# Moving one chunk's refinement, attention and third norm into the gate stage, with the gates' PSUM banks shared out anew

## The reference, cut to what matters

```python
x = x + tanh(g_xattn[0]) * attention16heads(layernorm(x), ctx)        # 1st norm
n = layernorm(x)                                                       # 2nd norm of the code: norm 1
integrated, v = n, 0
for _ in range(2):                                                     # it = 0, 1
    h = gelu([integrated, v] @ w1 + b1)        # 8 experts of 64, and a shared one
    a, b, g = split(h @ w2 + b2)               # for the shared and the two chosen experts
    v_next = sigmoid(a) * v - softplus(b) * (integrated - mu)
    x_next = integrated + 0.1 * sigmoid(g) * v_next
    (weighted over shared, first, second; then mixed in by halt)
refined = gelu(integrated @ refine_w1 + b) @ refine_w2 + b
x = x + tanh(g_ffn[0]) * (n + integration_weight * refined)
n = layernorm(x)                                                       # norm 2
x = x + tanh(g_xattn[1]) * softmax(n @ ctx.T) @ ctx                    # one head, per sequence
n = layernorm(x)                                                       # norm 3
top2 experts of 8 by n @ Wr + br; x = x + tanh(g_ffn[1]) * sum_k w_k * (silu(n@W1+b1) * (n@W2+b2)) @ W3 + b3
```

## Time and profile before

| | |
|---|---|
| median of 3 runs | 653.5 us (652.99 to 660.25) |
| the profiled execution's own time | 653.35 us |
| its span | 651.5 us |
| TensorE matmuls busy | 567.6 us, 87% |
| VectorE busy | 431.5 us, 66% |
| ScalarE busy | 307.7 us, 47% |
| GpSimd busy | 205.1 us, 31% |
| mean granted TensorE clock | 0.925 of full |

### The profile page before, as it was taken

One profiled execution on the slowest core, in us unless ns is written; L12 is line 12 of the kernel. 1 busy time (PEld: TensorE's weight loads), 2 busy tenths in 40 slices (PEclk: granted clock), 3 DMA queues, 4 the chain that ended last, 5 costly groups with the idle time before them and its releaser, 6 DMA issues.

```text
span 651.5 us, 9912 instructions
## 1 busy us (share of the span) xinstructions
PE 567.6 (87%) x3307; PEld 339.3 (52%) x3318; DVE 431.5 (66%) x1054; ACT 307.7 (47%) x630; POOL 205.1 (31%) x214
## 2 busy tenths in 40 slices
PE   3777799898898689899999999999767498999994
PEld 2433434444453234344444444445646498999993
DVE  3778858888438888877624567676767754454455
ACT  2544446565667653445445244362634244444431
POOL 3909500101012679100572000001046673333330
PEclk9795869999999989899999999999888599999996
DMA  8595880000019700000004000000202399999966
GB/s 252 149 186 104 150 183 14 2 4 3 2 63 309 248 0 1 2 0 0 0 1 129 0 1 1 0 2 0 16 12 83 116 304 305 323 328 321 345 210 202
DMA packets 53894, 71.14 MB, mean 109 GB/s; under 512 B 11484, under 2 KB 41508, under 8 KB 53556
## 3 DMA queue, kind: packets, MB, share of 16 engines
q1 hardware_dynamic: 50852, 65.55, 35.0%
q0 software_dynamic: 2272, 4.69, 1.9%
q10 hardware_dynamic: 720, 0.27, 0.2%
HBM read 59.12 MB, written 21.29 MB: 123 GB/s over the span
## 4 chain that ended last, share of the span: by engine, by line
PE 42%; DVE 9%; SPq 7%; issue 3%; DMA 3%; ACT 2%; POOL 0%; POOLq 0%; DVEq 0%; ACTq 0%
PE psum L1871 19%; PE psum L2099 5%; PE psum L1800 3%; PE psum L1802 3%; SPq L571 2%; PE psum L1868 2%; PE psum L2110 2%; DMA wb<-in_wall_dram 2%; DVE hidden L1238 1%; PE psum L1960 1%; SPq L587 1%; SPq L581 1%; PE psum L1924 1%; SPq L578 1%; PE psum L1869 1%
## 5 line engine op out<-in xcount | busy, mean ns | idle before, releaser
L1871 PE MATMUL psum<-hidden,ew 128*128 128x512 f32 x320 | 145.5, 598 | 0.5
L830 ACT ACTIVATE probs<-psum 128x512 f32<-128x512 f32 x128 | 72.7, 596 | 60.9 <-PE psum L1659 60.2
L1871 PEld LDWEIGHTS psum<-hidden,ew 128*128 128x128 f32 x320 | 61.4, 192 | 71.7 <-issue 70.5
L1097 DVE TENSOR_REDUCE negmax<-psum 128x4 f32<-128x1024 f32 x64 | 77.0, 1218 | 23.0 <-PE psum L1636 22.8
L1566 DVE SCALAR_TENSOR_TENSOR gated<-psum,wb,silu_g 128x128 f32<-128x128 f32 x156 | 43.9, 345 | 54.6 <-ACT silu_g L1017 53.0
L2099 PE MATMUL psum<-xbT,wb 128*128 128x128 f32 x624 | 78.2, 280 | 0.8 <-DMA wb<-in_wall_dram 0.5
L2099 PEld LDWEIGHTS psum<-xbT,wb 128*128 128x128 f32 x624 | 74.4, 195 | 1.9 <-DMA wb<-in_wall_dram 1.2
L1017 ACT ACTIVATE silu_g<-psum,wb 128x128 f32<-128x128 f32 x156 | 44.5, 368 | 58.4 <-PE psum L2099 58.4
L773 POOL DMA_INDIRECT sorted_y<-yb,xb x39 | 37.2, 953 | 65.1 <-DVE yb L1558 63.6
L1659 PE MATMUL psum<-stacks 50*128 50x256 bf16 x256 | 49.5, 295 | 9.2 <-ACT probs L830 3.9
L631 POOL TENSOR_SCALAR rstd<-meanvar 128x4 f32<-128x4 f32 x16 | 4.9, 306 | 166.7 <-DVE meanvar L1035 166.6
(11 more groups left out here) (253 smaller groups left out, 994.4 us busy)
## 6 DMA issues: line engine op xcount, KB each, us to landing
wb<-in_wall_dram SPq DMA_DIRECT2D x39, 516.0 KB, 4.7
wb<-in_wall_dram SPq DMA_DIRECT2D x39, 256.0 KB, 4.9
sorted_x<-in_slots_dram SPq DMA_DIRECT2D x1, 9815.0 KB, 32.2
stacks<-stacked SPq DMA_DIRECT2D x12, 384.0 KB, 8.3
xb<-sorted_x SPq DMA_DIRECT2D x39, 65.0 KB, 3.7
stacked<-parts SPq DMA_DIRECT2D x6, 384.0 KB, 3.4
back<-sorted_y SPq DMA_DIRECT2D x8, 256.0 KB, 4.4
stacked<-parts SPq DMA_DIRECT2D x6, 256.0 KB, 3.4
```

Source lines behind the costliest of these rows:

```text
L830: nc.scalar.activation(probs[:, g % 2, h % 4, :, :], s2[n % 2].rearrange("p (k q) -> p k q", k=2), ACT.Exp, scale=float(HD) ** -0.5).then_ ...
L1097: nc.vector.tensor_reduce(negmax[:, p].rearrange("p h q -> p (h q)"), psum[:, i:i + 2, :].rearrange("p h (q k) -> p (h q) k", q=2), AX.X, ...
L1871: last = nc.tensor.matmul(dst, ew2[:, j, cols], hidden[:, k - 1, j, c, :], start=False, stop=(j == 3))
```

## The change

Norm 3 of chunk 0 now comes ahead of norm 2 of chunk 1 (`TURNS`). In the second iteration:

- `refine_up(0)` goes behind part 5 of chunk 1's gates, its Gelus to the start of chunk 2 on ScalarE, `refine_down(0)` between the soft units 1 and 2 of chunk 2, the rest of norm 2, the transposes and both scores of chunk 0 among the gates of chunk 2, and its maxima just ahead of the last two passes of `second_step(2)`.
- The transposes of chunk 0's probabilities stand behind soft units 1 and 2 of chunk 3, `weigh_context(0)` and (1) behind gate part 1, `rows_to_columns(0)` behind part 4. `refine_up(1)` and `refine_down(1)` stay behind parts 0 and 2; `second_columns(1)` behind part 5.
- The soft units of the second iteration have two banks, 2 and 3, and unit `u` waits for `soft_done` of unit `u - 2`. Bank 4 takes chunk 0's transposed probabilities, its attention output and its rows.
- The list behind the loop is shorter and in another order; VectorE's `choose(1)` goes ahead of `layer_norm_apply(2)`.
- The hidden units lie by chunk, so that the later stages' memory can be loaded once chunks 0 and 1 are through their gates; `wo` moves behind `attnT`; SyncE waits for four more semaphores ahead of the first expert's weights.

```diff
-TURNS = ((2, 0), (2, 1), (3, 0), (3, 1), (2, 2), (2, 3), (3, 2), (3, 3))
+TURNS = ((2, 0), (3, 0), (2, 1), (3, 1), (2, 2), (2, 3), (3, 2), (3, 3))
...
-        hidden = sm("hidden", [P, 2, 4, NC, CH])
+        hidden = sm("hidden", [P, NC, 2, 4, CH])
...
             if part == "up":
-                return bank[(0 if c < 2 else 6) + m]
+                return bank[m if c < 2 else (6, 2)[m]]
...
+        def soft_bank(it, c, k):
+
+            return bank[2 + (3 * c + k) % (2 if it else 3)]
+
+        def fused_bank(b):
+
+            return bank[4][:, b * 2 * D:(b + 1) * 2 * D] if b < 2 else bank[4 + b % 2][:, 0:2 * D]
+
+        def rows_bank(c):
+
+            return bank[(4, 5, 6, 6)[c]]
...
@@ SyncE
-            sp.wait_ge(gate_psum, gate_use(1, NC))
+            sp.wait_ge(gate_psum, gate_use(1, 2))
...
+            sp.wait_ge(gate_psum, gate_use(1, NC))
+            sp.wait_ge(state_ready, 2 * NC)
+            sp.wait_ge(refine_h_ready, 2 * NC)
+            sp.wait_ge(refined_psum, NC)
             sp.wait_ge(early_ready, 1)
             load_weights(0)
...
@@ GpSimd
             rstd_of_chunk(2, 0)
+            rstd_of_chunk(3, 0)
             rstd_of_chunk(2, 1)
...
+            rstd_of_chunk(3, 1)
+            send_rows(0, range(0, 2))
             rstd_of_chunk(2, 2)
-            send_rows(0, range(0, 4))
+            send_rows(0, range(2, 5))
             rstd_of_chunk(2, 3)
-            send_rows(0, range(4, GR))
-            send_rows(1, range(0, 3))
+            send_rows(0, range(5, GR))
+            send_rows(1, range(0, 5))
             rstd_of_chunk(3, 2)
-            send_rows(1, range(3, 6))
+            send_rows(1, range(5, GR))
             rstd_of_chunk(3, 3)
-            send_rows(1, range(6, GR))
...
@@ ScalarE
+                    if it and c == L and k == 1:
+                        copy_probsT(0)
...
-                    if it and c == L and i in (3, 5):
-                        copy_xT2(i // 5)
+                    if it and c == 2 and i == 3:
+                        copy_xT2(0)
+                    if it and c == L and i == 4:
+                        copy_xT3(0)
+                        copy_rows(0)
+                    if it and c == L and i == 5:
+                        copy_xT2(1)
...
-                    if it and c == L:
+                    if it and c == 2:
                         refine_gelus(0)
                     nc.scalar.preload_act_table_set("natural_log_exp_and_others")
+                    if it and c == L:
+                        exps2(0)
+                        exps2(1)
                     softplus(it, c)
                     if it and c == L:
+                        copy_probsT(1)
                         refine_gelus(1)
                     sigmoids(it, c)
...
@@ VectorE, second_step
-                if c == L:
+                if c == 2:
                     layer_norm_apply(0, turn(2, 0))
-                    add_refined(1)
                 for k in range(3):
+                    if c == L and k == 1:
+                        sums_of(0)
+                        fuse(0)
+                        fuse(1)
+                        third_stats(0)
                     dve.wait_ge(sigmoid_done, gate_use(1, c) + 2 + k)
...
                 if c == L:
-                    layer_norm_apply(1, turn(2, 1))
+                    add_refined(1)
+                    layer_norm_rows(0)
                 for k in range(3):
-                    if c == L and k:
-                        maxima2(k - 1)
+                    if c == L and k == 1:
+                        layer_norm_apply(1, turn(2, 1))
+                    if c == L and k == 2:
+                        maxima2(2)
+                        maxima2(3)
                     dve.wait_ge(sigmoid_done, gate_use(1, c) + 5 + k)
...
-                if c == L:
-                    maxima2(2)
-                    sums_of(0)
-                    maxima2(3)
+                if c == 2:
+                    maxima2(0)
+                    maxima2(1)
...
@@ VectorE, behind the loop
-            fuse(0)
-            fuse(1)
-            third_stats(0)
+            choose(0)
             sums_of(1)
             fuse(2)
-            layer_norm_rows(0)
             fuse(3)
             third_stats(1)
-            add_refined(2)
-            choose(0)
-            layer_norm_rows(1)
             weights_of(0)
             slots_of(0)
+            layer_norm_rows(1)
+            add_refined(2)
             add_refined(3)
+            choose(1)
             layer_norm_apply(2, turn(2, 2))
-            choose(1)
             maxima2(4)
...
@@ TensorE, soft_parts
-                    if u >= 3:
+                    if it and 3 * c + k >= 2:
+                        pe.wait_ge(soft_done, u - 1)
+                    elif u >= 3:
                         pe.wait_ge(soft_done, u - 2)
-                    controller(bank[2 + u % 3][:], k, 1, c).then_inc(soft_psum, 1)
-                    if it and c == L and k == 0:
-                        refine_up(0)
-                if it and c == L:
-                    refine_down(0)
+                    controller(soft_bank(it, c, k)[:], k, 1, c).then_inc(soft_psum, 1)
+                    if it and c == 2 and k == 1:
+                        refine_down(0)
+                    if it and c == L and k:
+                        transpose_probs(k - 1)
...
@@ TensorE, gate_parts
+                    if it and c == 1 and i == 5:
+                        refine_up(0)
+                    if it and c == 2:
+                        if i == 3:
+                            second_columns(0)
+                        if i == 5:
+                            second_scores(0)
+                            second_scores(1)
                     if it and c == L:
                         if i == 0:
                             refine_up(1)
+                        if i == 1:
+                            weigh_context(0)
+                            weigh_context(1)
                         if i == 2:
                             refine_down(1)
-                        if i == 3:
-                            second_columns(0)
                         if i == 4:
-                            second_scores(0)
+                            rows_to_columns(0)
                         if i == 5:
                             second_columns(1)
...
@@ TensorE, behind the loop
-            second_scores(1)
             second_scores(2)
-            transpose_probs(0)
             second_scores(3)
-            transpose_probs(1)
-            weigh_context(0)
-            weigh_context(1)
+            route_logits(0)
             transpose_probs(2)
-            refine_up(2)
             transpose_probs(3)
             weigh_context(2)
             weigh_context(3)
+            refine_up(2)
+            route_ranks(0)
             refine_down(2)
             refine_up(3)
-            rows_to_columns(0)
-            route_logits(0)
+            rows_to_columns(1)
+            route_logits(1)
             refine_down(3)
-            rows_to_columns(1)
-            route_ranks(0)
-            route_logits(1)
             second_columns(2)
```

More of the change, by code:

```diff
@@ L841, in first_gelu @@
                 if j < 4:
-                    nc.scalar.activation(hidden[:, 1, j, c, :], bank[m % 2][:], ACT.Gelu, bias=eb1[:, j:j + 1]).then_inc(gelu_done, 1)
+                    nc.scalar.activation(hidden[:, c, 1, j, :], bank[m % 2][:], ACT.Gelu, bias=eb1[:, j:j + 1]).then_inc(gelu_done, 1)
                 else:
@@ L931, in copy_xT3 @@
                 act.wait_ge(xT_psum, turn(3, c))
-                nc.scalar.copy(xT[:, chunk(c)], bank[6][:]).then_inc(xT_ready, 1)
+                nc.scalar.copy(xT[:, chunk(c)], rows_bank(c)[:]).then_inc(xT_ready, 1)
             def copy_rows(c):
@@ L956, in copy_probsT @@
                     act.wait_ge(fused_psum, b - 1)
-                nc.scalar.copy(probsT[:, b % 2, :, :].rearrange("p k q -> p (k q)"), bank[2][:]).then_inc(probsT_ready, 1)
+                nc.scalar.copy(probsT[:, b % 2, :, :].rearrange("p k q -> p (k q)"), bank[4 if b < 2 else 2][:]).then_inc(probsT_ready, 1)
             for it in range(2):
@@ L1376, in sums_of, with fuse, third_stats @@
                 steps.wait()
+            def fuse(b):
+                dve.wait_ge(fused_psum, 2 if b < 2 else b + 1)
+                for q in range(2):
+                    xt = x[:, 2 * b + q, :]
+                    last = nc.vector.scalar_tensor_tensor(xt, fused_bank(b)[:, q * D:(q + 1) * D], sums2[:, b, q:q + 1], xt, ALU.mult, ALU.add)
+                last.then_inc(x3_ready, 1)
+            def third_stats(c):
+                dve.wait_ge(x3_ready, 2 * c + 2)
+                layer_norm_stats(c)
             for it in range(2):
@@ L1870, in controller @@
                 for j in range(4):
-                    last = nc.tensor.matmul(dst, ew2[:, j, cols], hidden[:, k - 1, j, c, :], start=False, stop=(j == 3))
```

(20 more changed lines are left out.)

74 lines of the change are left out of this document (37 added, 37 removed).

## The result

| | before | changed |
|---|---|---|
| median of 4 runs each | 653.25 us (647.56 to 660.25) | 673.52 us (667.73 to 675.85) |
| ratio, 95% interval | | 1.0304 (1.0254 to 1.0354) |
| profiled execution, its span | 653.35, 651.5 us | 671.59, 669.8 us |
| mean granted TensorE clock | 0.925 | 0.916 |

The change makes the kernel 3% slower. TensorE's timeline dates the stages of both profiled executions: the gate stage of the second iteration goes from the first soft part of chunk 0 to the end of the last gate part, the tail from there to second_columns(2).

What follows compares the result with a forecast made beforehand. It took TensorE, busy almost without a break, to bound the second iteration's gate stage. 11.75 + 3.95 + 5.1 + 4.0 - 0.4 - 6.4 = +18.0 on 653.35 gave 671.4 us, range 661 to 677.

Steps and rivals of the forecast that it cites:

- part 1: Second iteration's gate stage: with two banks, unit 2 of each chunk waits for VectorE's second pass over unit 0; +11.75 us.
- part 2: Chunk 3's gates: rows_to_columns(0) waits for VectorE's layer_norm_rows(0), which comes after gate 2 and add_refined(1); +3.95 us.
- part 3: Matmuls behind the three longest new TensorE waits run partly at the lower clock, 1.7 us each; +5.1 us.
- part 5: Tail from last gate part to second_columns(2) shrinks from 30.8 to 24.4 us, with choose(1) on the path; -6.4 us.
- part 4: Work newly moved into the gate stage (scores, transposes, weigh_context, rows_to_columns(0)) adds 4.0 us; small gaps gone, -0.4.
- edits at nothing: GpSimd's send order, SyncE's earlier loads and new waits, moved wo and hidden units: 0, at most a few tenths.
- clock holds: Rival: all waits in the gate stage come, but none lowers the clock in what follows; 666.3 us, chance 0.17.
- only bank waits: Rival: chunk 3's extra VectorE passes find slack, so its waits and their clock drops vanish; 659.4 us, chance 0.09.
- not slower: Rival: the second pass over unit 0 is over before unit 1 is, so no bank waits; 650.6 us, chance 0.06.
- the tail did shrink: Denies the rival that the tail up to second_columns(2) keeps its length, its gain eaten; 677.8 us, chance 0.11.

Runs made afterwards that it cites:

- e2: Changed kernel with three banks for the soft units in chunks 0 to 2 and two in chunk 3; ratio to before 1.0094.
- e3: Changed kernel with layer_norm_rows(0) moved ahead of the third gate pass of chunk 3 on VectorE; ratio to before 1.0256.
- e9: Changed kernel with three banks throughout, layer_norm_rows(0) and add_refined(1) ahead of chunk 3's third gate pass, and choose(1) behind layer_norm_apply(2); ratio to before 0.9917.
- e5b: Changed kernel with 7 unused filler matmuls in each of three TensorE waits (unit 2 of chunks 1 and 3, rows_to_columns(0)); ratio to before 1.0222.
- e5: Changed kernel with 14 unused filler matmuls in each of three TensorE waits (unit 2 of chunks 1 and 3, rows_to_columns(0)); ratio to before 1.0256.
- e6: Changed kernel with choose(1) back behind layer_norm_apply(2) on VectorE; ratio to before 1.0266.
- e10: Kernel before with only the new SBUF places (hidden units kept by chunk, wo behind attnT); ratio to before 1.0014.
- e0: Changed kernel itself, run again on the chip of the experiments; ratio to before 1.0371.
- e7: Changed kernel with three banks for the soft units in all chunks, chunk 0's attention using banks of units already read; ratio to before 1.0007.
- e11: e9 with add_refined(2) ahead of weights_of(0) on VectorE and refine_down(3) ahead of rows_to_columns(1) on TensorE; ratio to before 0.9934.

## Why the prediction was right

The forecast was 671.4 us; the profiled execution took 671.59, the median was 673.52. That the profiled execution lies 0.2 us from the forecast is luck: the four executions go from 667.73 to 675.85, and differences of -0.5 (part 1), -0.3 (part 2), +0.7 (part 3), +1.3 (part 5) and -0.8 (outside the sum) nearly cancel. What held is the mechanism, term by term:

| term | predicted | measured |
|---|---|---|
| part 1, chunk 0 | 1.7 | 1.6 |
| part 1, chunk 1 | 3.6 | 3.54 |
| part 1, chunk 2 | 1.85 | 1.76 |
| part 1, chunk 3 | 4.6 | 4.3 |
| part 2, rows | 3.95 | 3.70 |
| part 3, clock | 5.1 | 5.8 |
| part 4, work moved in, less gaps | 3.6 | 3.5 (what is left) |
| part 5, tail | -6.4 | -5.1 |
| not in the sum: start, to block, blocks | 0 | -0.8 |
| sum | 18.0 | 18.3 |

- Part 1 is shown from both sides: two banks put into before cost 13.95, three put back in chunks 0 to 2 gave 8.25, and in all chunks 13.97 (134.77 - 120.80), the clock's share included in all three. It worked because VectorE's and ScalarE's rows already gave the end of the wait, and only its beginning was new.
- Of the two rules that the prediction weighed (the Trainium skill, Perfetto Trace Analysis), that of the section Matmuls held: independent groups that no longer rotate through enough banks waited for the read-out. The other rule (section Matmul Optimizations) doesn't stand against it here as the prediction had it: by the kernel's text bank 4 is empty in chunks 0 to 2 of the changed kernel, and using it there gave the 8.25 of e2, so for these chunks both rules ask for the same.
- Part 2 is right in place and size (3.70 for 3.95). e3 and e9 show that the rows can be ready in time, and e3 that this alone gives 1.6.
- Part 3 was taken three times at one row's 1.7, and so was too small by 0.7; it measured 5.35 - 3.65 = 1.70 at chunk 1, 6.02 - 3.65 = 2.37 at chunk 3, and behind the rows 4.88 - 3.65 and 0.90 - 0.44, 1.7. e5b took 5.7 away by keeping TensorE busy, the whole of the measured 5.8. One reading was off: that the clock stayed at 1.00 behind the 1.51 us ahead of 470.87 isn't shown by 468 to 471, which ends 0.13 us behind that start; 471 to 474, at 1.00 too, shows it.
- Part 4: 24.19 less the waits (11.2 + 3.7) and the clock (5.8) leaves 3.5. This is a remainder and no measurement of its own.
- Part 5 is off by 1.3. refine_down(3) took 3.23 us where I had put 1.78, at a clock of 0.58 from 495 to 498: 1.45 more. I had reckoned with the lower clock only in the rival. In e2, e3 and e5, where it took 2.03, the tail is 24.8. The 25.7 also lies above the 24 to 25 that the prediction named as its sign. The rest of the working holds: e6 shows choose(1) on the path (25.68 to 23.45, 2.2 for 2.25).
- The edits at nothing: nothing, by e10 for the places. The sends' and the loads' new times were not tried alone; "to block" at 32.12 says that they held up nothing before the blocks. The 1.7 more from the first block on is not the change's for all that is shown: in e0 the same stretch took 132.15, in before 132.23.
- The rivals: clock holds is refuted by the three windows; only bank waits, by the 0.93, 2.98 and 3.54 that stayed in e2; not slower, by the waits; the tail did shrink.

What the prediction didn't ask was whether the idea or its banks were at fault. With its banks given back (e7) the move is worth nothing; with VectorE's order put right as well (e9) it pays: +3.5 for the work among the gates, 2.6 us of waits, and a tail 7.7 shorter, 2.9 less in the three stages. The bank lent cost 14.0, several times that gain.

## What to carry to other kernels

When a change takes a buffer out of a rotation, look in the trace for the row that reads the buffer last, and compare its end with the start of the instruction that will now reuse it; every microsecond between them is a wait if that engine sets the pace, and all that is queued behind it waits too. On TensorE, add what the lower clock costs behind a wait, from a row of the same kernel, and look for free buffers among those already read (here the units' own) before lending one that is still in use. After taking a wait away, ask what is late next: the second wait may stand right behind the first and have been hidden by it.

## What the runs showed of the hardware that was not expected

- The same wait has different prices: behind 3.38 us of idling the unit took 5.35 us, behind 0.93 and 2.98 with four transposes between them 6.02, and in e2, at the same place with the same brackets, 5.15 (428.91 to 434.06). Behind the rows it is the other way round: the nine matmuls took 4.88 us in changed and 6.13 in e2 (454.28 to 460.41), behind a wait of 3.54 in both.
- refine_down(3) ran slow (3.23 us) in the changed kernel, where no single gap ahead of it was over 1.1 us, but there were several; TensorE was busy for 1.67 us of the three from 492 to 495:

```profile
492.00:495.00 3.00, 1.67 (x13) 1.44 (x14) 2.51 (x12) 1.39 (x3) 2.15 (x4) 1.00 0.13 44
495.00:498.00 3.00, 3.00 (x17) 2.83 (x16) 0.00 (x0) 0.00 (x0) 2.50 (x3) 0.58 0.05 17
```

In e11, with fewer gaps ahead of it, it took 2.02. In e2, whose tail has the order of changed, the slow matmuls came earlier, in weigh_context(2) and (3), which took 3.30 us there (469.74 to 473.04, clock 0.51 from 470 to 473) and 1.83 in changed (483.23 to 485.06), and refine_down(3) was fast. So where the lower clock falls can shift from one execution to another in the same order of work. TensorE's timeline of e2:

```profile
453.37 1.11 PE L2048 MATMUL psum<-ident,xp 128*128 128x128 f32 x4 [3.54 <-DVE xp L1077]
...
454.70 5.87 PE L1902 MATMUL psum<-hidden,ew 128*128 128x512 f32 x8
...
469.74 3.47 PE L2036 MATMUL psum<-chosen,probsT 128*128 128x128 f32 x16
...
481.70 2.03 PE L1979 MATMUL psum<-fw,unmasked 128*128 128x128 f32 x16
```
